# Feed-forward stage: half of the next tile's transposes inside the third bank's products, and the first add ahead of the second low part

## What is computed

```
h = concatenate([state_space_kernel(x), txt], axis=1)      # (16, 205, 1024)
h = h + attention(layernorm(h)) @ Wo                       # 32 heads, causal, ALiBi
y = layernorm(h)
h = h + y @ base_W.T + base_b                              # 1024 -> 1024
      + 2 * sum over experts of (y @ A_e.T) * w_e @ B_e.T  # 8 experts of rank 16
```

## Time and profile before

| | us |
|---|---|
| median of 3 runs (lowest, highest) | 1736.79 (1732.65, 1740.34) |
| the profiled execution's own time | 1738.08 |
| its span | 1736.3 |
| TensorE busy in the span | 1507.8 |
| VectorE busy | 1134.3 |
| ScalarE busy | 737.2 |
| GpSimd busy | 536.6 |

### The profile page before, as it was taken

The page is one execution under the profiler, slowest core; times in us unless marked ns, Lnnn a source line. Parts: engine busy times, 40 slices in busy tenths (PEclk is TensorE's granted clock), DMA queues, the critical chain, the costliest instruction groups (busy, mean ns, idle before and its releaser), DMA issues. The chain is left out here.

```text
span 1736.3 us, 31628 instructions
## 1 busy us (share of the span) xinstructions
PE 1507.8 (87%) x9700; PEld 1335.7 (77%) x9700; DVE 1134.3 (65%) x4142; ACT 737.2 (42%) x2624; POOL 536.6 (31%) x314
## 2 busy tenths in 40 slices
PE   0355399989999999999999769999999999999999
PEld 0355288878878787887888558888988888888887
DVE  7999378879788878879787854443444434344343
ACT  3455157777767767767878631011000010100100
POOL 1788314443534343443445400110101111010110
PEclk9877689999999999989999679999999999999999
DMA  6144455454554445445455341212112121211201
GB/s 200 37 89 93 103 98 109 80 83 96 80 103 73 104 72 108 73 75 100 79 117 88 103 171 47 73 37 72 48 60 72 36 72 40 69 66 43 73 32 40
DMA packets 110527, 139.63 MB, mean 80 GB/s; under 512 B 13156, under 2 KB 96484, under 8 KB 110040
## 3 DMA queue, kind: packets, MB, share of 16 engines
q1 hardware_dynamic: 110408, 138.41, 34.8%
HBM read 62.82 MB, written 40.30 MB: 59 GB/s over the span
## 5 line engine op out<-in xcount | busy, mean ns | idle before, releaser
L700 ACT ACTIVATE P<-P,nmax 128x128 f32<-128x128 f32 (+1 forms) x1024 | 434.3, 426 | 95.1 <-DVE nmax L790 88.9
L764 POOL TENSOR_TENSOR P<-P,rden 128x512 f32<-128x512 f32 (+1 forms) x256 | 329.2, 1308 | 451.5 <-DVE rden L796 451.4
L790 DVE CUSTOM_DVE_ANT_0 P<-sc,mask 128x128 f32<-128x128 f32 (+1 forms) x1024 | 292.4, 323 | 101.1 <-PE sc L612 94.7
L1126 POOL TENSOR_TENSOR h<-h,base_b 128x1024 f32<-128x1024 f32 (+1 forms) x26 | 84.2, 3240 | 637.4 <-DVE xn L1153 637.4
L642 PE MATMUL pr<-xT_hi,wq_hi 128*128 128x410 f32 x576 | 243.0, 422 | 0.0
L802 DVE COPY PTR<-pt 128x282 f32<-128x282 f32 x512 | 222.2, 435 | 30.3 <-PE pt L622 17.1
L1039 PE MATMUL b<-w_hi,x2T_hi 128*128 128x390 f32 (+3 forms) x624 | 214.8, 344 | 14.3 <-DVE h L1199 13.2
L1039 PE MATMUL b<-w_lo,x2T_hi 128*128 128x390 f32 (+3 forms) x624 | 212.4, 340 | 0.0
L1039 PE MATMUL b<-w_hi,x2T_lo 128*128 128x390 f32 (+3 forms) x624 | 212.0, 340 | 0.0
L642 PE MATMUL pr<-xT_lo,wq_hi 128*128 128x410 f32 x576 | 204.0, 354 | 0.0
L642 PE MATMUL pr<-xT_hi,wq_lo 128*128 128x410 f32 x576 | 202.9, 352 | 0.0
(11 more groups left out here) (174 smaller groups left out, 3049.1 us busy)
## 6 DMA issues: line engine op xcount, KB each, us to landing
Qs<-q_hi SPq DMA_DIRECT2D x128, 205.0 KB, 4.5
Qs<-q_lo SPq DMA_DIRECT2D x64, 205.0 KB, 5.5
att_dram<-att SPq DMA_DIRECT2D x64, 205.0 KB, 2.4
at<-att_dram SPq DMA_DIRECT2D x25, 512.0 KB, 4.6
h<-h_dram SPq DMA_DIRECT2D x25, 512.0 KB, 3.4
out<-h SPq DMA_DIRECT2D x25, 512.0 KB, 2.6
h_dram<-Y SPq DMA_DIRECT2D x64, 128.0 KB, 3.0
ht<-h_dram SPq DMA_DIRECT2D x16, 512.0 KB, 5.8
```

What stands on the lines that cost most here:

```text
L700: last = nc.scalar.activation(P[rows, j % 2, i, cols], P[rows, j % 2, i, cols], ACT.Exp, scale=-1.0, bias=nmax[at], accum_out=den[at])
L764: lastp = nc.gpsimd.tensor_tensor(w, w, r, ALU.mult)
L790: lastv = v.tensor_tensor_reduce(P[0:n, j % 2, i, cols], sc[i % 2][0:n, cols], mask[0:n, m], 1.0, 3.0e38, ALU.add, ALU.min, nmax[0:n, j % ...
L1126: nc.gpsimd.tensor_tensor(h2[0:n, par, :], h2[0:n, par, :], base_b[0:n, :], ALU.add).then_inc(biased, 1)
```

## The change

Two orders are altered; no operation is added or taken away.

On TensorE `transpose_x` makes one half only, and is called twice: half 0 inside bank 2's products, ahead of piece 5 (`TURN_AT = 5`, so 15 products come before it and 9 after), half 1 where all eight stood before. The wait for `x_ready` goes with half 0.

On VectorE the order after `residual_ln` becomes: low half 0 of the next tile, add of bank 0 (posts `first_read`), low half 1, adds of banks 1 and 2 (the last posts `out_ready`), and then the low part of the attention input of tile t+2.

```diff
+    TURN_AT = 5
...
-            def three(bank, n, lhs, w, cols, K, start=True, stop=True, between=None, reopen=False):
+            def three(bank, n, lhs, w, cols, K, start=True, stop=True, between=None, between_at=KC // 2, reopen=False):
                 for k in range(K):
-                    if k == K // 2 and between is not None:
+                    if k == between_at and between is not None:
                         between()
...
-            def transpose_x(t, n):
-                pe.wait_ge(x_ready, t + 1)
-                wait_count(pe, xT_lo, 2 * t)
-                for half in range(2):
-                    for q in range(4):
-                        last = nc.tensor.transpose(x_ps[half][:, 128 * q:128 * q + n], xn[0:n, (4 * half + q) * 128:(4 * half + q + 1) * 128], ident[0:n, 0:n])
-                    last.then_inc(xT_done, 1)
+            def transpose_x(t, n, half):
+                if half == 0:
+                    pe.wait_ge(x_ready, t + 1)
+                    wait_count(pe, xT_lo, 2 * t)
+                for q in range(4):
+                    last = nc.tensor.transpose(x_ps[half][:, 128 * q:128 * q + n], xn[0:n, (4 * half + q) * 128:(4 * half + q + 1) * 128], ident[0:n, 0:n])
+                last.then_inc(xT_done, 1)
...
-                three(base_ps[2], n, xT, w2, slice(*CHUNKS[2]), KC, stop=False)
+                three(base_ps[2], n, xT, w2, slice(*CHUNKS[2]), KC, stop=False, between_at=TURN_AT,
+                      between=(lambda: transpose_x(t + 1, n1, 0)) if n1 else None)
                 if n1:
-                    transpose_x(t + 1, n1)
+                    transpose_x(t + 1, n1, 1)
...
+                if n1:
+                    x_lo(t + 1, n1, 0)
+                dve.wait_ge(biased, t + 1)
+                add_base(t, par, n, 0).then_inc(first_read, 1)
+                if n1:
+                    x_lo(t + 1, n1, 1)
+                add_base(t, par, n, 1)
+                add_base(t, par, n, 2).then_inc(out_ready, 1)
                 if n2:
                     att_lo(t + 2, par, n2)
-                if n1:
-                    x_lo(t + 1, n1)
-                dve.wait_ge(biased, t + 1)
-                for i, (bank, (at_col, cols)) in enumerate(zip(base_ps, OUT_AT)):
-                    dve.wait_ge(base_done, 3 * t + i + 1)
-                    last = v.tensor_tensor(h2[0:n, par, cols], bank[0:n, at_col:at_col + cols.stop - cols.start], h2[0:n, par, cols], ALU.add)
-                    if i == 0:
-                        last.then_inc(first_read, 1)
-                last.then_inc(out_ready, 1)
```

More of the change, by code:

```diff
@@ L1087, in _ @@
             attn_out(1, 1, 128)
-            transpose_x(0, 128)
+            transpose_x(0, 128, 0)
+            transpose_x(0, 128, 1)
             visit(pe, body)
@@ L1157, in att_lo, with x_lo, add_base @@
                 v.tensor_tensor(aT[1][:, par, :, 0:n], at[:, par, :, 0:n], aT[0][:, par, :, 0:n].bitcast(F32), ALU.subtract).then_inc(a_lo, 1)
[L1159 to L1164, removed]
+            def x_lo(t, n, half):
+                dve.wait_ge(xT_hi, 2 * t + half + 1)
+                src = x_ps[half][:, :].rearrange("p (q t) -> p q t", q=4)[:, :, 0:n]
+                c = slice(4 * half, 4 * half + 4)
+                v.tensor_tensor(xT[1][:, c, 0:n], src, xT[0][:, c, 0:n].bitcast(F32), ALU.subtract).then_inc(xT_lo, 1)
+            def add_base(t, par, n, i):
+                at_col, cols = OUT_AT[i]
+                dve.wait_ge(base_done, 3 * t + i + 1)
+                return v.tensor_tensor(h2[0:n, par, cols], base_ps[i][0:n, at_col:at_col + cols.stop - cols.start], h2[0:n, par, cols], ALU.add)
             def router(t, n, link):
@@ L1217, in _ @@
                     residual_ln(0, 0, 0, 128, Chain(dve, chain))
-            x_lo(0, 128)
+            x_lo(0, 128, 0)
+            x_lo(0, 128, 1)
             visit(dve, body)
```

## The result

The changed kernel takes 1720.81 us (median of 6 runs, 1719.61 to 1724.64); the kernel before, in as many runs beside it, 1738.17 us (1732.65 to 1740.34). The ratio is 0.9908, 95% interval 0.9891 to 0.9925: faster by 0.9%, or 17.4 us by the medians. The forecast, taken off the median of the three runs then shown, was 1719.6 us, a change of -17.2.

The account below looks back on a forecast made before the run. TensorE's own stream was taken to bound the feed-forward stage. Steady edges -18.8 us and tile 0 +1.6 gave -17.2, which taken off the 1736.79 us median predicts 1719.6 us, range 1714.5 to 1727.

Parts of the forecast that it names:

- What bounds the stage: Feed-forward stage: TensorE, busy 320.1 of 327 us, sets the time; only its stands, 13.2 us in 23 waits, can be won.
- One edge loses 0.82 us, 23 of them 18.8: Steady tile edges: 0.74 us stand plus 0.07 us slow restart on TensorE vanish at each, 18.8 us less.
- What comes late next: VectorE after the first add: the moved attention low part ends at 1229.95, its reader comes at 1232.04, 2 us of cover.
- The split costs nothing: TensorE, bank 2: making the eight transposes in two groups costs 0, at most 2.1 us over 23 tiles.
- Tile 0 pays 1.6: Tile 0: nine products move behind the wait for xn and run at the lower clock, net 1.6 us more.
- The last edge: nothing: Edge to the last tile, of 80 tokens: its stand is shorter, so its gain is counted as nothing.
- The first add is still late: Steady edges: wake and add each 0.25 us longer leave 0.3 us of each stand, 6.9 us, time 1726.5; chance 0.09.
- The loop edge shows: Ten runtime-loop edges on TensorE: 0.46 us each costs 4.6, time 1724.2; at 0.74 each, 1727.0; chance 0.07.
- Slower by the turn wait: Wait for xn inside bank 2: xn later by 1.4 us makes the kernel 0.5% slower, time 1745.5; chance 0.04.

Follow-up runs that it names:

- the runs with half of the change: Two runs, each with one engine's new order against the kernel before: TensorE's split transposes only, 1736.17 us; VectorE's new order only, 1723.30 us.
- the kernel with tile 0 excepted: The changed kernel, but in tile 0 all eight transposes stay behind bank 2: 1718.72 us, and 1722.07 us when run once more.
- VectorE's half alone: Against the kernel before, only VectorE's new order, with all eight transposes still behind bank 2: 1723.30 us, ratio 0.9919.
- the run at piece 4: The changed kernel with its four early transposes three products earlier, ahead of piece 4 instead of 5 (`TURN_AT = 4`): 1731.94 us.

## Why the prediction was right

**What bounds the stage** was read rightly: TensorE's own stream, with one stand per tile.

**One edge loses 0.82 us, 23 of them 18.8** (exactly 18.9, a slip of 0.1). Measured 0.861 a tile, 19.8. The stand and the restart went as computed (0.74 and 0.06 to 0.07). The rest, 0.04 to 0.07, lies mostly in bank 1, whose 24 products take 4.24 us in the changed kernel against 4.29 before; in the runs with half of the change they take 4.24 to 4.30. I didn't forecast it and no run names its cause.

**What comes late next.** As computed: the attention low part ends at 1228.15 + 1.21 = 1229.36, and its reader, TensorE's first attention product, starts at 1231.45. That is 2.1 us of cover, where the forecast had 2.

**The split costs nothing.** Bank 2's 24 products, eight transposes and first three low-rank products together took 4.25 + 0.79 + 0.43 = 5.47 us before, and 2.68 + 0.35 + 1.67 + 0.35 + 0.42 = 5.47 after. Right, and the upper bound of 2.1 us wasn't needed.

**Tile 0 pays 1.6.** It paid 1.53, and by the mechanism given. TensorE's timeline at its end, and a window behind the stand:

```profile
1063.23 1.01 PE L1063 MATMUL x<-ident,xn 128*128 128x128 f32 x4 [4.02 <-DVE xn L1156]
1063.90 0.67 PE L1040 MATMUL b<-w_hi,x2T_hi 128*128 128x388 f32 x1
1064.37 0.53 PE L1040 MATMUL b<-w_lo,x2T_hi 128*128 128x388 f32 x1
...
1066.89 0.60 PE L1063 MATMUL x<-ident,xn 128*128 128x128 f32 x4
1067.24 0.36 PE L1040 MATMUL b<-wq_hi,zT_hi 128*128 128x246 f32 x1
...
1068.75 0.34 PE L1040 MATMUL b<-w_hi,x2T_hi 128*128 128x390 f32 x1
```

```profile
1064.23:1065.23 1.00, 1.00 (x5) 1.00 (x4) 0.31 (x1) 0.60 (x1) 1.00 (x1) 0.50 0.00 0
```

A stand of 4.02 us inside bank 2; nine products from 1063.90 to 1066.89, 2.99 us against the 2.97 of the sum; four transposes in 0.35; the low-rank products 1.51 against 1.50. One thing the sum took as given was chance: it set the slow work behind the shorter stand against the slow work behind the longer, and in the kernel with tile 0 excepted the former was fast. Measured against that, the split in tile 0 costs 3.0 us (21.1 against 18.1).

**The last edge: nothing.** It gave 0.24.

**The rivals.** *The first add is still late*: at 22 of 23 edges it isn't. At the edge from tile 23 to tile 24 it is. TensorE and then VectorE there:

```profile
1674.65 0.28 PE L1040 MATMUL b<-wq_hi,zT_lo 128*128 128x246 f32 x1
...
1675.66 0.34 PE L1040 MATMUL b<-wq_hi,zT_lo 128*128 128x388 f32 x1
1675.96 0.42 PE L1040 MATMUL b<-w_hi,x2T_hi 128*128 128x390 f32 x1
```

```profile
1675.40 0.41 DVE L1171 TENSOR_TENSOR h<-b,h 128x246 f32<-128x246 f32 x1 [1.47 <-PE b L1040]
```

The third product of bank 0 has drained at 1674.93, the add starts 0.47 us later instead of 0.02 to 0.03, and TensorE's next tile starts 0.30 us after the last product instead of 0.18. The slack of 0.32 us is spent, 0.19 us lost with the restart. VectorE did nothing else in that time. The same edge shows it in every kernel that has both halves of the change and the loop (eight profiles), except the one with the attention low part moved back; with the loop written out it is gone. So it hangs on where an instruction stands in VectorE's stream, not on data. One thing goes with it. The changed kernel's DMA queues from 1676 to 1678 have

```profile
q14 instruction: 1, 0.01, 1.5%
```

a packet of instructions at 1676.06, 0.66 us behind the start of the late add, and each of the eight profiles has one 0.66 to 0.69 us behind it. With the attention low part moved back, the packet comes 0.30 us into that attention low part instead, where VectorE has work that covers a delay; with the loop written out, none comes within 10 us of this edge. In VectorE's half alone it comes 0.63 us behind the same add, and nothing is late, since a low half runs directly ahead of the add. So the late add seems to stand where VectorE's stream comes to new code (that q14 brings VectorE's code is read from these coincidences alone). The written-out loop doesn't rule this cause out; it shows that such places mostly cost nothing. No run shows that it is the cause. *The loop edge shows*: no, all ten lie at 0.17 or 0.18 us, and the written-out loop is no faster. *Slower by the turn wait*: no, but the run at piece 4 shows that the danger was real, and sized as said: 0.23 us of slack against three products of 0.18 left 0.30 us of stand, and 9.1 us of the gain went.

The sum's small misses all have one sign: 1.0 us more was won at the edges, 0.24 at the last, and tile 0 paid 0.07 less. Together the stage won 18.5 us where the sum has 17.2, and that agreement within 1.3 us is the mechanism. The earlier stages scatter by several us, so that the measured change came to 17.4, closer still, and the time within 1.2 us, is partly luck.

## What to carry to other kernels

Where an engine stands for a chain over several others, write the chain down with the slot at which the engine would be ready, and look first for a link that is queued behind work its waiter doesn't need: here one add moved ahead of one conversion gave four fifths of the gain without touching TensorE, while starting the chain earlier gave by itself 4.5 us in the steady tiles and lost 2.1 of them in tile 0. A wait that is moved ahead of work which used to stand in front of it takes that cover away, and one pays for it where the wait is long; treat the first pass, whose cover is missing, as a case of its own (3 us here). Read a stage's gain between two instructions of the profile when the untouched stages scatter by more than the gain.

## What was not expected of the hardware

- GpSimd's 128x1024 add of two SBUF inputs takes 2.39 us, and 3.29 to 3.31 with VectorE's subtraction of two SBUF inputs of the same size beside it. VectorE's subtraction hardly moves, 1.21 against 1.22 us.
- Behind stands of the same 2.43 or 2.44 us the granted clock fell to 0.50 in three profiles and stayed at 1.00 in two. With the stand filled by products it stayed in all three profiles.
- The 24 products of 390 columns of bank 1 take 4.24 to 4.30 us at a granted clock of 1.00: 4.24 in every steady tile of the changed kernel, mostly 4.29 in the kernel before.
- One add on VectorE started 0.47 us after its product had drained instead of 0.03, in eight profiles of kernels with the same loop, with a packet of instructions 0.66 to 0.69 us behind its start each time.
